# Moving the first MLP chunk's projection, normalisation and turns into the last attention group

## The reference, cut to what matters

```python
mod = jax.nn.swish(c) @ w_mod + b_mod                       # six vectors for each batch
xn = _ln(x) * (1 + sc_msa) + sh_msa
q, k, v = heads(xn @ w_qkv + b_qkv);  q, k = _ln(q, g_q), _ln(k, g_k)
o = softmax(q @ k.T * HD ** -0.5) @ v                       # per batch and head, 2048 x 2048
x = x + g_msa * (o @ w_proj + b_proj)
xn2 = _ln(x) * (1 + sc_mlp) + sh_mlp
x = x + g_mlp * (gelu(xn2 @ w1 + b1) @ w2 + b2)
```

## Time and profile before

| | us |
|---|---|
| median of 3 runs (2844.62 to 2847.23) | 2846.82 |
| the profiled execution | 2848.59 |
| its span in the trace | 2846.8 |
| attention ends, `project(0, 0)` begins, at | 1839.57 |
| `up(0)` begins at | 1867.66 |
| `down(0)` ends at | 1993.82 |
| TensorE busy | 2769.0 (97%) |
| VectorE busy | 1988.7 (70%) |
| ScalarE busy | 1523.3 (54%) |
| GpSimd busy | 713.6 (25%) |

### The profile page before, as it was taken

The page is one execution under the profiler, slowest core; times in us unless marked ns, Lnnn a source line. Parts: engine busy times, 40 slices in busy tenths (PEclk is TensorE's granted clock), DMA queues, the critical chain, the costliest instruction groups (busy, mean ns, idle before and its releaser), DMA issues.

```text
span 2846.8 us, 43086 instructions
## 1 busy us (share of the span) xinstructions
PE 2769.0 (97%) x14754; PEld 1434.0 (50%) x14754; DVE 1988.7 (70%) x2663; ACT 1523.3 (54%) x2232; POOL 713.6 (25%) x540
## 2 busy tenths in 40 slices
PE   6699999999999999999999999989999999999999
PEld 3344444444444444444444444447576675756656
DVE  6588998888888888888888899853535344353421
ACT  4567777788877777777777777631211112111110
POOL 1433476622233333333333311010000000000000
PEclk9899999999999999999999999989999999999999
DMA  7422232222211122222223223130110202112000
GB/s 217 87 50 50 50 96 73 78 58 52 52 34 30 30 64 59 75 67 73 72 74 77 58 79 133 63 120 23 67 65 26 85 6 89 32 58 67 23 18 17
DMA packets 236397, 181.22 MB, mean 64 GB/s; under 512 B 149175, under 2 KB 185469, under 8 KB 235557
## 3 DMA queue, kind: packets, MB, share of 16 engines
q1 hardware_dynamic: 235974, 179.31, 22.9%
q10 hardware_dynamic: 288, 0.04, 0.0%
HBM read 99.70 MB, written 46.04 MB: 51 GB/s over the span
## 4 chain that ended last, share of the span: by engine, by line
PE 91%; DVE 4%; POOL 1%; ACT 1%; issue 1%; SPq 1%; DMA 1%; ACTq 0%; DVEq 0%
PE at_ps L1623 19%; PE at_ps L1647 15%; PE at_ps L1052 15%; PE at_ps L1049 15%; PE at_ps L1040 14%; PE at_ps L1070 10%; DVE at_plo L846 2%; PE at_ps L1105 1%; PE at_ps L1613 1%; ACT at_p L671 1%; DMA st_wm_first<-in_L_cond_b_mod 0%; PE at_ps L208 0%; POOL at_tssq L545 0%; PE at_ps L1081 0%; PE at_ps L1092 0%
## 5 line engine op out<-in xcount | busy, mean ns | idle before, releaser
L846 DVE TENSOR_TENSOR at_plo<-at_p 128x1024 fp32r<-128x1024 f32 x1024 | 1273.6, 1264 | 191.9 <-ACT at_p L671 184.6
L671 ACT ACTIVATE at_p<-at_ps 128x1024 f32<-128x1024 f32 x1024 | 1047.0, 1025 | 401.5 <-PE at_ps L1040 401.0
L1052 PE MATMUL at_ps<-at_plo,at_vr 128*37 128x512 f32 x2048 | 1074.2, 592 | 0.0
L1049 PE MATMUL at_ps<-at_p,at_v 128*73 128x512 bf16 x2048 | 797.8, 390 | 6.0 <-DVE at_plo L846 5.9
L1623 PE MATMUL at_ps<-ml_w2s,ml_hid 128*128 128x288 f16 x3456 | 428.1, 286 | 2.0 <-issue 2.0
L1647 PE MATMUL at_ps<-ml_xhi,ml_w 128*128 128x512 f16 x1296 | 399.3, 381 | 3.5 <-issue 3.5
L1623 PEld LDWEIGHTS at_ps<-ml_w2s,ml_hid 128*128 128x128 f16 x3456 | 338.0, 98 | 87.0 <-issue 2.5
L1049 PEld LDWEIGHTS at_ps<-at_p,at_v 128*73 128x73 f16 x2048 | 233.3, 114 | 247.4 <-issue 9.1
L1052 PEld LDWEIGHTS at_ps<-at_plo,at_vr 128*37 128x37 f32 x2048 | 234.3, 114 | 222.5 <-issue 1.2
L543 POOL TENSOR_TENSOR at_tssq<-at_tssq,head_eps 128x8 f32<-128x8 f32 x112 | 124.5, 1111 | 840.6 <-DVE at_tssq L816 840.6
L1040 PE MATMUL at_ps<-at_qk_even 109*128 (+1 forms) x1024 | 311.2, 385 | 14.5 <-ACT at_p L671 7.4
(11 more groups left out here) (170 smaller groups left out, 2303.1 us busy)
## 6 DMA issues: line engine op xcount, KB each, us to landing
head_sums<-at_oT SPq DMA_DIRECT2D x256, 72.0 KB
ml_held<-head_sums SPq DMA_DIRECT2D x64, 256.0 KB
at_xy<-in_L_cond_w SPq DMA_DIRECT2D x34, 288.0 KB
w_halves<-at_wq SPq DMA_DIRECT2D x68, 144.0 KB
at_xy<-in_x SPq DMA_DIRECT2D x32, 288.0 KB, 2.8
ml_x<-in_x SPq DMA_DIRECT2D x8, 1152.0 KB, 5.6
out<-ml_x SPq DMA_DIRECT2D x7, 1152.0 KB, 4.5
ml_held<-head_rden SPq DMA_DIRECT2D x24, 216.0 KB
```

The costliest lines, as they stand in the source:

```text
L671: act.activation(p[:, s % NP, :], ps[:, 2 * (s % 2):2 * (s % 2) + 2, :].rearrange("p a n -> p (a n)"), ACT.Exp).then_inc(exp_done, 1)
L846: nc.vector.tensor_tensor(plo[:, s % NP, :], p[:, s % NP, :], high, ALU.subtract).then_inc(plo_ready, 1)
L1049: nc.tensor.matmul(acc[0:VW, bass.ds((U % 2) * CH, CH)], v16[:, h % 2, 2 * s + a, 0:VW], high, start=(s == 0 and a == 0), stop=False, skip ...
L1052: last = nc.tensor.matmul(acc[0:RW, bass.ds((U % 2) * CH, CH)], vr[:, h % 2, 2 * s + a, 0:RW], plo[:, s % NP, a * CH:(a + 1) * CH], start= ...
```

## The change

The work between attention and `up(0)` is moved into units 9 to 14 of group 7, in which TensorE's loop is now written out unit by unit.

- TensorE: tile i of the projection is done in unit 9 + i, its 14 products in pieces of 3, 3, 2, 2, 2, 2 after steps 2 to 7 (`tensor_early`), into banks 6 and 7. The 5 turns stand in unit 14 after steps 0, 1, 3, 4 and 6. `up(0)` follows the last unit directly.
- VectorE: gate of tile i at step 7 of unit 9 + i; adding x, statistics, their aggregation and normalising at steps 0, 1, 2 and 5 of unit 10 + i; `low_x` of slices 0 to 3 in unit 14, of slice 4 at the start of unit 15.
- ScalarE: `affine(0)` in unit 14. Its high half is now made by GpSimd (`first_high`), for chunk 0 alone.
- GpSimd: the additions of the slices (`add_o` for chunk 0) move to it from VectorE, in units 4 to 8; the powers, the five high halves, and then its additions of the gate's bias to x.
- The slices are loaded in units 3 to 7 (before: 3 to 12), the gates in unit 1 (before: 7), w1 in unit 8 (before: 5). Multiplication, high and low half of the slices go to units 4 to 9 (before: 6 to 15).
- SyncE, after attention: the storing of batch 1's inverted denominators and the wait for it move from ahead of the sums of chunk 1 to behind them. VectorE inverts after `hidden` of block f = 9 of `up(0)`.

```diff
-    SUMS_AT, ADD_IN, MULTIPLY_IN, HIGH_IN, LOW_IN = ({u0 + 2 * k: k for k in range(KC)} for u0 in (4, 5, 6, 7, 7))
+    SUMS_AT, ADD_IN, MULTIPLY_IN, HIGH_IN, LOW_IN = ({u0 + k: k for k in range(KC)} for u0 in (3, 4, 4, 4, 5))
+    PROJECT_IN = {9 + i: i for i in range(TPC)}
+    PROJECT_AT = (None, None, (0, 3), (3, 6), (6, 8), (8, 10), (10, 12), (12, 14))
+    NORMAL_IN = {10 + i: i for i in range(TPC)}
+    TURN_IN = 14
...
@@ sync_early
+            sp.dma_start(self.gates[:, :, :, :].rearrange("p b v n -> p (b v n)"), bcast(self.gates_dram, 0, P)).then_inc(self.gates_loaded, 16)
...
-        if u == 5:
+        if u == 8:
             self.load_w1(sp)
...
@@ sync
         self.load_den(sp, 1)
         self.load_w2(sp)
-        self.store_rden(sp, 1)
-        sp.wait_ge(self.rden_stored, 16 * B)
         sp.wait_ge(self.xt_ready, KC)
         self.load_sums(sp, 1, (0, 1))
         for J in range(self.CHUNKS - 1):
             self.load_x(sp, J + 1)
             self.load_sums(sp, J + 1, (2, 3, 4))
+            if J == 0:
+                self.store_rden(sp, 1)
+                sp.wait_ge(self.rden_stored, 16 * B)
...
+    def gpsimd_early(self, pool, u):
+        if u in self.ADD_IN:
+            k = self.ADD_IN[u]
+            pool.wait_ge(self.held_loaded[k % 2], 16 * self.so_far[k])
+            pool.tensor_tensor(self.total(k), self.total(k), self.slot[:, k % 2, 1, :], ALU.add).then_inc(self.added, 1)
+        if u == self.TURN_IN:
+            for k in range(KC):
+                self.first_high(pool, k)
...
+    def tensor_early(self, pe, u, s):
+        if u in self.PROJECT_IN and self.PROJECT_AT[s]:
+            i, (n0, n1) = self.PROJECT_IN[u], self.PROJECT_AT[s]
...
+            for n in range(n0, n1):
+                l, w = ops[n]
+                for half in range(2):
+                    last = self.nc.tensor.matmul(self.early_pair[:, half, :], l, w[:, half * HALF:(half + 1) * HALF],
+                                                 start=(n == 0), stop=(n == len(ops) - 1))
...
+        if u == self.TURN_IN and s in self.TURN_AT:
...
+            self.turn_y(pe, 0, (self.TURN_AT[s],))
...
-        project(0, 0)
-        turn_y(0, range(KC))
         for J in range(self.CHUNKS):
```

More of the change, by code:

```diff
@@ L1203, in _ @@
                     pe.nop()
+                if G == GROUPS - 1:
+                    for u in range(UNITS):
+                        attend(G, u // NCH, u % NCH)
+                    continue
                 for h in range(GH):
@@ L1468, in scalar @@
             if more:
-                affine(J + 1)
+                for k in range(KC):
+                    self.affine(act, J + 1, k)
     def add_o(self, dve, J, k):
@@ new lines, in vector_early @@
+        if u in self.PROJECT_IN and s == 7:
+            i = self.PROJECT_IN[u]
+            self.gate_part(dve, i, i, self.early_pair, 0, 0)
+        if u in self.NORMAL_IN:
+            i = self.NORMAL_IN[u]
+            if s == 0:
+                self.add_part(dve, 0, i, i, self.x1_ready)
+            if s == 1:
+                dve.wait_ge(self.x1_ready, i + 1)
+                for h in range(2):
+                    last = self.nc.vector.bn_stats(self.stats[:, i, h, :], self.x1[:, i, h * HALF:(h + 1) * HALF])
+                last.then_inc(self.first_stats, 1)
+            if s == 2:
+                dve.wait_ge(self.first_stats, i + 1)
+                self.nc.vector.bn_aggr(self.mv[:, i, :], self.stats[:, i, :, :].rearrange("p a b -> p (a b)")).then_inc(self.first_mv, 1)
+            if s == 5:
+                dve.wait_ge(self.first_rstd, i + 1)
+                row = self.x1[:, i, :]
+                for c0, c1, at in ((0, H, 0), (KF * P, H, H)):
+                    last = self.nc.vector.tensor_scalar(self.tok[:, i, at:at + c1 - c0], row[:, c0:c1], self.mv[:, i, 0:1],
+                                                        self.rstd[:, 1, i:i + 1], ALU.subtract, ALU.mult)
+                if i == TPC - 1:
+                    last.then_inc(self.y_ready, 1)
@@ new lines, in vector_early, with gate_part @@
+        if u == self.TURN_IN and s in self.LOW_X_AT:
+            self.low_x(dve, 0, self.LOW_X_AT[s])
+        if u == self.TURN_IN + 1 and s == 0:
+            self.low_x(dve, 0, KF)
+    def gate_part(self, dve, i, r, pair, b, v):
+        dve.wait_ge(self.pair_ready, r + 1)
+        gate = self.gates[:, b, v, :].rearrange("p (h n) -> p h n", h=2)
+        self.nc.vector.tensor_tensor(self.part[:, i % 2, :].rearrange("p (h n) -> p h n", h=2), pair, gate, ALU.mult).then_inc(self.pair_taken, 1)
@@ new lines, in add_part, with low_x @@
+    def add_part(self, dve, J, i, r, after):
+        row = self.x1[:, (J % 2) * TPC + i, :]
+        dve.wait_ge(self.pair_taken, r + 1)
+        self.nc.vector.tensor_tensor(row, row, self.part[:, i % 2, :], ALU.add).then_inc(after, 1)
+    def low_x(self, dve, J, k):
+        rows = P if k < KF else KT
+        dve.wait_ge(self.xhi_ready, J * KC + k + 1)
+        self.nc.vector.tensor_tensor(self.xlo[0:rows, k, :], self.aff[0:rows, k % 2, :], self.xhi[0:rows, k, :], ALU.subtract).then_inc(self.xlo_ready, 1)
@@ L1505, in residual @@
         def residual(J, i, r, v, after):
-            row = self.x1[:, (J % 2) * TPC + i, :]
-            dve.wait_ge(self.pair_ready, r + 1)
-            gate = self.gates[:, J // NCH, v, :].rearrange("p (h n) -> p h n", h=2)
-            nc.vector.tensor_tensor(self.part[:, i % 2, :].rearrange("p (h n) -> p h n", h=2), self.pair(i), gate, ALU.mult).then_inc(self.pair_taken, 1)
-            dve.wait_ge(self.pair_taken, r + 1)
-            nc.vector.tensor_tensor(row, row, self.part[:, i % 2, :], ALU.add).then_inc(after, 1)
+            self.gate_part(dve, i, r, self.pair(i), J // NCH, v)
+            self.add_part(dve, J, i, r, after)
         def project(J, r0):
@@ L1581, in down @@
                 if turn:
-                    low_x(J + 1, self.WITH_DOWN[i])
-        nc.vector.memset(self.xlo[KT:P, KF, :], 0.0).then_inc(self.xlo_zero, 1)
-        dve.wait_ge(self.gates_loaded, 16)
-        first_project()
-        self.invert_den(dve, 1)
-        low_x(0, range(KC))
+                    for k in self.WITH_DOWN[i]:
+                        self.low_x(dve, J + 1, k)
         for J in range(self.CHUNKS):
```

128 lines of the change are left out of this document (63 added, 65 removed).

## The result

| | before | after |
|---|---|---|
| median of the runs | 2846.38 us (6 runs, 2844.62 to 2847.23) | 2858.80 us (6 runs, 2857.48 to 2861.47) |
| profiled execution, span | 2848.59 us, 2846.8 us | 2861.47 us, 2859.7 us |
| ratio after / before | | 1.0045, 95% interval 1.0035 to 1.0056 |

The changed kernel is 12.4 us **slower**, more than the 0.2% that can be told from no change. The forecast was 2852, its range 2841 to 2861.

A forecast was written before the change was run, and what follows sets the result against it. TensorE was taken to bound attention, with VectorE nearly full, and to be partly idle or slow in the transition. Terms -12.15 + 5.2 + 12.6 + 0 = +5.65 us gave 2852.5 by the median, stated as 2852; range 2841 to 2861.

The forecast's parts named there:

- the transition goes: Between attention and `up(0)`: 28.09 us go, 15.94 of projection and turns are added in attention; 12.15 us saved.
- the units' loss: Attention units 5 to 15 of group 7: VectorE work that the units do not cover loses 5.2 us, ends 1 and 10.
- I take a loss of 0.55 of GpSimd's own time: Late attention units: VectorE beside GpSimd was taken to lose 0.55 of the time GpSimd's operations need by themselves.
- The 0.4 that were to be saved: TensorE's idle 0.4 us beside the last head, saved as that head falls into unit 10.
- The second rival: Late attention units: each us of GpSimd's work costs VectorE a whole one; 6 us more, 2858.5 us, chance 0.12.
- the stop: In `up(0)`: chunk 1's first sums queue behind w2, so TensorE idles after five blocks; 12.6 us lost, from 11.0 to 14.7.
- S = T + 24.8: Chunk 1's slice 0 is there 24.8 us after `up(0)` starts, from 23.2 to 26.9.
- The next slices are wanted 9 us apart and take 4 each: covered: In `up(0)`: chunk 1's slices after slice 0 arrive in time and cost nothing more.
- Clock 0: In `up(0)`: 2.93 us of low clock are paid after the idle time, not at the start; net 0, from -1.4 to +1.
- Inversion and chunks 1 to 7, nothing: The inversion at f = 9 of `up(0)` has 1.9 us to spare; chunks 1 to 7 keep their order; no cost.
- The likeliest case: The whole kernel: the forecast itself, +5.65 us, chance 0.70, its own range 2845 to 2858 us.

## Why the prediction was right or wrong

By its own sum, -12.15 + 5.2 + 12.6 + 0 = +5.65. Measured, in the same terms: -12.15 + 10.9 + 14.65 - 0.53 = **+12.87**.

- **-12.15, the transition goes**: right. No gap stood ahead of `up(0)`; units 10 to 12 took 14.0, 14.3 and 14.4 us, where 14.4 was forecast, and unit 9 took 15.0.
- **+5.2, the units' loss: the term that was mis-sized**. It measured 10.9, outside the term's own ends of 1 and 10. The step that failed is "I take a loss of 0.55 of GpSimd's own time". Where VectorE ran without a gap, each addition cost it 1.1 or 1.22 us, 0.9 of GpSimd's own time, and each conversion 0.4 of 0.61. In units 5 to 8 the forecast was 2.0; units 4 to 7 measured 5.1, of which 4.1 in unit 6. For unit 15 it was 2.1 + 1.5; measured 5.1, and 0.5 when GpSimd's additions were taken out. The 0.4 that were to be saved weren't seen: units 8 to 14 together lost 0.8. The 0.55 came from two rows. In the earlier trace rows `low_x` ran with gaps, and GpSimd's additions partly fell into them: the three grew by 0.05, 0.53 and 1.01 us, and the row gives their mean. In the earlier trace rows the loss of 1.9 us for a head was right, and the head of unit 6 cost 2.0; but it was set against an estimate of 3.1 us for all of the head's operations, and so hid what a single two-input operation costs, 1.06 us in that stretch. A rate from a stretch with gaps isn't the rate where there are none.
- **A link that the sum did not have**: the lag of VectorE was weighed against TensorE's need of the low halves alone. In unit 6 it also reached TensorE through the high half in ScalarE's queue, 1.93 us of standing.
- **The second rival**, that each us of GpSimd's costs VectorE a whole one, had 11.2 us of loss and 2858.5 us against 10.9 and 2858.8. It was given 0.12, with "the measured rates" against it; the rule of the Trainium skill that stood beside it described this kernel better than the rate that I took. That its time came out within 0.3 us is in part luck: it has 1.4 us in unit 14 that were not lost, and a stop of 12.6 us that took 14.65.
- **+12.6, the stop**: the mechanism was right in each link (the wait of slice 0's addition, the high half behind it, Gelu 3, five blocks, then the stop), 14.65 us measured, inside the bounds of 11.0 to 14.7 at their upper end. The step that was short is S = T + 24.8; the addition ran at 1893.63, T + 27.2. w2 was not later than forecast: its second half was issued at 1870.17 and took 16.8 us, so it landed at T + 20.6, forecast T + 22.1. Slice 0 came 6.6 us behind it, forecast 2.7. The working let slice 0's transfers alone pass behind w2. SyncE had issued those of slice 1 from 1883.29 on and the rows of x at 1887.04, and the DMA share was 0.95 over the whole stop; that these took the time is my reading, no run parts it. TensorE resumed at S + 2.72, forecast S + 2.95.
- **"The next slices are wanted 9 us apart and take 4 each: covered"** held, but only as the first stop had already let w2 pass. With slice 0 ahead of w2 it was slice 2 that stopped TensorE.
- **Clock 0**: 2.93 us of low clock before, 2.40 after, net -0.5; inside the bounds.
- **Inversion and chunks 1 to 7, nothing**: right.

The range held the result. The likeliest case's own range ends at "some +12" on 2846.82, which is 2858.8 and was written as 2858: the result lies on its edge, since the forecast's stop and the second rival's loss came true together. The range ought to have reached over their sum. And slower, with 0.41, stood behind the same, with 0.45, for that one rate.

## What to carry to other kernels

When work moves forward, ask of every load whose cover is now gone what lies ahead of it in its queue, and follow it to the last slice: w2 cost nothing for as long as 28 us of transition stood before `up(0)`, and 17 after; to move the sums of two slices ahead of it gained 6.6 us, to move all the loads that were wanted sooner 19.5. Work given to GpSimd is not free beside a VectorE that is full: count its whole time against VectorE, and look whether VectorE would do it in less (0.69 us against 1.1 lost). Look also at what stands behind a small operation that waits for the loaded engine: the high half held up exponentials, and an addition held up a head. And take the price of two engines' meeting from a stretch with no gaps, or measure it by a probe.
